# Layer 1 steps: parts split in fewer operations, sums on GpSimd, scalings on ScalarE, VectorE's additions in other steps

## What is computed

```
x = x + gb0 * gate * expert_out[slot]                      # end of layer 0
h = layernorm(x) * (1 + ca) + sa
k, v, q = split(h @ w_in);  a = softmax(q k^T / sqrt(8) + bias(rel. position)) v     # first attention, 16 heads
a, g = split(a @ w_gate + b_gate);  x = x + ga * a * sigmoid(g)
h = layernorm(x) * (1 + cb) + sb                           # the middle norm
h = h + mla(rmsnorm(h, g1))                                # second attention: causal, 16 heads, latent 64
h = h + moe(rmsnorm(h, g2))                                # top 2 of 8 experts
x = x + gb * h
```

## Time and profile before

| | us |
|---|---|
| median of three runs | 1864.76 (1862.15 to 1874.69) |
| the profiled execution | 1861.73 |
| its span, first to last instruction | 1860.0 |
| layer 1's first row minimum, stretch s = 0 | 693.1 |
| start of stretches s = 1 to 7 | 761.7, 840.8, 942.6, 1058.1, 1176.8, 1305.1, 1440.7 |
| last tile of stream 0 | 1570.7 |

### The profile page before, as it was taken

The page is one execution under the profiler, slowest core; times in us unless marked ns, Lnnn a source line. Parts: engine busy times, 40 slices in busy tenths (PEclk is TensorE's granted clock), DMA queues, the critical chain, the costliest instruction groups (busy, mean ns, idle before and its releaser), DMA issues.

```text
span 1860.0 us, 50554 instructions
## 1 busy us (share of the span) xinstructions
PE 1617.7 (87%) x19264; PEld 1179.7 (63%) x19264; DVE 1326.5 (71%) x4176; ACT 1007.1 (54%) x2196; POOL 779.3 (42%) x1021
## 2 busy tenths in 40 slices
PE   3899898899883939989999999989999988888887
PEld 2677676777772727766666666656767766544545
DVE  6678777876761127788778798897886786685646
ACT  1545454455451316665666667666666656564532
POOL 3111311220115237786656566565464574243210
PEclk7899999999995969999999999999999999988999
DMA  3631122122004424344423325143452333535321
GB/s 111 190 94 46 40 84 65 36 69 82 5 7 122 157 81 155 131 151 151 160 64 128 125 84 164 56 147 98 131 161 88 114 127 111 161 98 162 109 62 53
DMA packets 143839, 194.53 MB, mean 105 GB/s; under 512 B 21920, under 2 KB 110176, under 8 KB 142320
## 3 DMA queue, kind: packets, MB, share of 16 engines
q1 hardware_dynamic: 129312, 171.75, 29.6%
q0 software_dynamic: 5760, 14.03, 2.4%
q10 hardware_dynamic: 8528, 5.51, 1.0%
HBM read 142.39 MB, written 50.69 MB: 104 GB/s over the span
## 4 chain that ended last, share of the span: by engine, by line
PE 44%; DVE 9%; issue 7%; ACT 5%; DMA 1%; POOL 1%; SPq 0%; another core or an unknown queue 0%; ACTq 0%; POOLq 0%; DVEq 0%
PE ps L2350 9%; PE ps L2333 7%; PE ps L2384 6%; PE ps L2394 3%; DVE l_XY L2601 3%; PE ps L2361 3%; ACT PT L2162 2%; PE ps L1229 2%; PE ps L2484 2%; PE ps L1238 2%; PE ps L2459 2%; PE ps L2410 2%; DVE ps L2601 1%; PE ps L2431 1%; PE ps L2522 1%
## 5 line engine op out<-in xcount | busy, mean ns | idle before, releaser
L2053 POOL TENSOR_SCALAR l_XY<-l_XY,l_nmax 128x512 f32<-128x512 f32 x512 | 374.9, 737 | 295.9 <-DVE l_nmax L2601 287.6
L2601 DVE CUSTOM_DVE_ANT_0 l_XY<-ps,strips 128x512 f32<-128x512 f32 x512 | 347.7, 687 | 170.4 <-PE ps L2333 115.2
L2162 ACT ACTIVATE PT<-ps 128x512 f32<-128x512 f32 x512 | 307.3, 601 | 248.0 <-PE ps L2350 236.3
L2333 PE MATMUL ps<-l_stack 72*128 72x512 bf16 (+3 forms) x1024 | 350.9, 348 | 50.1 <-DVE l_nmax L2601 35.5
L2350 PE MATMUL ps<-ident,l_XY 128*128 128x128 f32 x2048 | 320.6, 279 | 1.7 <-ACT PT L2162 1.4
L2350 PEld LDWEIGHTS ps<-ident,l_XY 128*128 128x128 f32 x2048 | 236.9, 142 | 91.0 <-issue 56.8
L2601 DVE CUSTOM_DVE_ANT_0 ps<-ps,mask 128x384 f32<-128x384 f32 (+3 forms) x512 | 250.2, 496 | 24.3 <-PE ps L2333 20.2
L2361 PE MATMUL ps<-l_stack 75*128 75x256 bf16 (+3 forms) x512 | 157.2, 308 | 22.0 <-ACT PT_odd L2165 7.5
L2333 PEld LDWEIGHTS ps<-l_stack 72*128 72x128 bf16 x1024 | 101.1, 99 | 100.5 <-DVE l_nmax L2601 55.7
L2384 PE MATMUL ps<-PT,v_aug 128*10 128x128 f32 x4096 | 137.6, 275 | 6.8 <-ACT l_O_sb L2171 6.4
L2165 ACT ACTIVATE PT_even<-ps 128x512 f32<-128x512 f32 (+1 forms) x256 | 125.1, 494 | 22.8 <-PE ps L2363 17.3
(11 more groups left out here) (372 smaller groups left out, 3215.9 us busy)
## 6 DMA issues: line engine op xcount, KB each, us to landing
l_stack<-parts_dram SPq DMA_DIRECT2D x384, 96.0 KB
strips<-bias_dram SPq DMA_DIRECT2D x16, 1792.0 KB
stack<-parts_dram SPq DMA_DIRECT2D x48, 384.0 KB
w_own<-table_dram SPq DMA_DIRECT2D x60, 256.0 KB
parts_dram<-l_parts SPq DMA_DIRECT2D x32, 384.0 KB
rows_dram<-mask SPq DMA_DIRECT2D x6, 2048.0 KB, 8.9
parts_dram<-parts SPq DMA_DIRECT2D x16, 384.0 KB, 6.5
x_b<-rows_dram SPq DMA_DIRECT2D x72, 64.0 KB
```

The source lines that it names most:

```text
L2053: nc.gpsimd.tensor_scalar(XY[:, c % XY_BUFS], XY[:, c % XY_BUFS], -1.0, nmax[:, c % 8:c % 8 + 1], ALU.mult, ALU.add).then_inc(y_pool, 1)
L2162: nc.scalar.activation(PT[:, u % QUADS, j], src.rearrange("p (k q) -> p k q", q=P), ACT.Exp).then_inc(moved, 1)
L2333: nc.tensor.matmul(ps[:, n % 3, 0:w], stack[0:STACK, 0, h, q * P:(q + 1) * P], stack[0:STACK, 1, h, 0:w], start=True, stop=True).then_inc( ...
L2601: nc.vector.tensor_tensor_reduce(out=dst, in0=src, in1=add, scale=-1.0, scalar=3.0e38, op0=ALU.add, op1=ALU.min, accum_out=low).then_inc(s ...
```

## The change

- `pre` gets its steps from a new function `pre_step`: y0 * gate * gb0 in two halves at i = 57 and 61 of the stretch before (-7 and -3), the sum into x at 0 on GpSimd (`x_added`), statistics at 5, variance at 9, the root at 10, the normalisation at 13, the turn at 15. Batch 1 has steps of its own, batch 0 runs ahead of the loop as before (`first_pre`).
- Splitting: VectorE's one subtraction writes part 1 in bf16 directly (for pre at 24 and 27, for mid at 49 and 53); the casts go. GpSimd makes the float difference itself and then part 2 (`last_part`, two operations, the second waiting for the first; for pre at 26 and 29, for mid at 51 and 55). Only the very first batch keeps the old form.
- `mid`: the sum into x at 27 goes to GpSimd (`x_gated`), VectorE waits for it at 29. The layer norm and its rows become two fused operations, (x - mean) * row at 33 and h * rstd + row at 37, each as four of 128x128; the one at 35 goes, and the root is waited for at 37. The scaling at 43 goes to ScalarE, four of 128x128.
- `router`: the scaling goes to ScalarE too (k = 13, four of 128x128; k = 11 for batches 4 and 5). In `MIXED_STAGES` add, square, variance and power come one step later, the plan's five steps at k = 45, 49, 53, 55, 57 (i = 25, 29, 33, 35, 37).
- SyncE loads the row gb0 of the batch after next at i = 20. Four semaphores of layer 0's experts, which end at 8 = E, serve the new waits.

```diff
@@ -1330,8 +1331,8 @@
-MIXED_STAGES = dict(wo=1, add=3, square=5, var=8, power=9, scale=15, turn=17, logits=19, top0=21, top1=25, both=25, gap=27, count=28,
-                    place=37, gates=37, scatter=38, plan=(50, 52, 54, 56, 58), fold=41)
+MIXED_STAGES = dict(wo=1, add=4, square=6, var=9, power=10, scale=13, turn=17, logits=19, top0=21, top1=25, both=25, gap=27, count=28,
+                    place=37, gates=37, scatter=38, plan=(45, 49, 53, 55, 57), fold=41)
@@ -1389,6 +1390,13 @@
 def router_steps(b):
     return max(routing(b)["fold"], routing(b)["plan"][-1]) + 1
+def pre_step(b, stage):
+    if b == 1:
+        return {"y0": 3, "y1": 5, "x": 7, "statistics": 9, "var": 11, "power": 12, "xn": 13, "split": 24}[stage]
+    return TILES * (b - 1) + {"y0": -7, "y1": -3, "x": 0, "statistics": 5, "var": 9, "power": 10, "xn": 13, "split": 24}[stage]
...
+MADE_AT = [(-1, ("xp", 0))] + [(pre_step(b, "xn"), ("xp", b)) for b in range(1, B)] + [
+ROOTS_AT = [(TILES * s + 43, ("xm", b)) for s, b in MID_OF.items()] + [(MOE_START[b] + routing(b)["scale"], ("xf", b)) for b in range(ROUTED)]
+TOKENS_SCALED = {what: n for n, (_, what) in enumerate(sorted(ROOTS_AT))}
+VARIANCE_AT = [(-1, (0, 0))] + [(pre_step(b, "var"), (0, b)) for b in range(1, B)] + [
...
@@ -1552,7 +1561,7 @@
-        for off, name in ((14, "xp"), (20, "pq"), (22, "pk"), (23, "pv")):
+        for off, name in ((15, "xp"), (20, "pq"), (22, "pk"), (23, "pv")):
@@ -1986,7 +1996,7 @@
-                    if pre is not None and pre < B - 1 and i == 60:
+                    if pre is not None and pre < B - 1 and i == 20:
@@ -2098,8 +2108,18 @@
                     nc.gpsimd.tensor_tensor(rows, rows, bc(b_gate_sb[:].unsqueeze(1), [P, 2, 2 * C]), ALU.add).then_inc(gated_ready, 1)
+                def x_added(b):
+                    pool.wait_ge(y_scaled, E + b)
+                    nc.gpsimd.tensor_tensor(x_rows(b), x_rows(b), y0[:], ALU.add).then_inc(x_in, 1)
+                def x_gated(b):
+                    pool.wait_ge(mid_sum, E + b + 1)
+                    nc.gpsimd.tensor_tensor(x_rows(b), x_rows(b), h_of(b), ALU.add).then_inc(x_mid, 1)
                 def last_part(k, a, b):
+                    if PART_NO[a, b]:
+                        order.link(nc.gpsimd.tensor_tensor(qk[:, k, :], qk[:, k, :], parts[:, k, 0, :], ALU.subtract))
@@ -2108,6 +2128,9 @@
                     last_part(k, 0, 0)
                 gather(1, range(TT))
+                    for b in range(1, B):
+                        if m == pre_step(b, "x"):
+                            x_added(b)
@@ -2115,8 +2138,10 @@
-                    if pre is not None and i == 10:
+                    if pre is not None and m == pre_step(pre, "power"):
+                    if mid is not None and i == 27:
+                        x_gated(mid)
@@ -2127,9 +2152,9 @@
                         if mid is not None and i == 19 + half_:
                             gate_sum(mid, half_)
-                        if pre is not None and i == 25 + 4 * k:
+                        if pre is not None and i == 26 + 3 * k:
-                        if mid is not None and i == 52 + 4 * k:
+                        if mid is not None and i == 51 + 4 * k:
@@ -2293,9 +2318,17 @@
                         evacuate(*what)
                     for what in outs_at(m):
+                    if s in MID_OF and i == 43:
+                        b = MID_OF[s]
+                        act.wait_ge(rstd_ready, VARIANCES[2, b] + 1)
+                        for t in range(TT):
+                            last = nc.scalar.activation(xn[:, t, :], h_of(b)[:, t, :], ACT.Copy, scale=rstd[2][:, t:t + 1])
+                        last.then_inc(tok_scaled, 1)
                     if s in MID_OF and i == 39:
+                        if ("xm", b) in XN_BEFORE:
+                            act.wait_ge(turned, XN_BEFORE["xm", b] + 1)
@@ -2307,6 +2340,11 @@
                         if k == routing(b)["gap"]:
                             gap_exponent(b)
+                        if k == routing(b)["scale"]:
+                            act.wait_ge(rstd_ready, VARIANCES[3, b] + 1)
+                            for t in range(TT):
+                                last = nc.scalar.activation(xf[:, t, :], h_of(b)[:, t, :], ACT.Copy, scale=rstd[3][:, t:t + 1])
+                            last.then_inc(tok_scaled, 1)
@@ -2421,7 +2459,10 @@
-                        pe.wait_ge(tok_ready, TOKENS_MADE[name, k] + 1)
+                        if (name, k) in TOKENS_SCALED:
+                            pe.wait_ge(tok_scaled, E + TOKENS_SCALED[name, k] + 1)
+                        else:
+                            pe.wait_ge(tok_ready, TOKENS_MADE[name, k] + 1)
@@ -2647,38 +2688,56 @@
                 def split(k, a, b, part):
 
                     if part == 0:
-                        s = PART_NO[a, b]
-                        link(nc.vector.tensor_tensor(qk[:, k, :], qk[:, k, :], parts[:, k, 0, :], ALU.subtract))
+                        if PART_NO[a, b]:
+                            nc.vector.tensor_tensor(parts[:, k, 1, :], qk[:, k, :], parts[:, k, 0, :], ALU.subtract).then_inc(second_part, 1)
+                        else:
+                            link(nc.vector.tensor_tensor(qk[:, k, :], qk[:, k, :], parts[:, k, 0, :], ALU.subtract))
-                def pre(b, i):
-                    if i == 3:
+                def scaled(b, half_):
+                    if half_ == 0:
-                        for t in range(TT):
-                            last = nc.vector.scalar_tensor_tensor(out=y0[:, t, :], in0=y0[:, t, :],
-                                                                  scalar=gate_keep[:, b * TT + t:b * TT + t + 1],
-                                                                  in1=gb0_now[:], op0=ALU.mult, op1=ALU.mult)
-                        link(last)
-                    if i == 7:
-                        linked()
-                        ins = nc.vector.tensor_tensor(x_rows(b), x_rows(b), y0[:], ALU.add)
-                        ins.then_inc(x_in, 1)
-                    if i == 9:
+                    for t in (2 * half_, 2 * half_ + 1):
+                        last = nc.vector.scalar_tensor_tensor(out=y0[:, t, :], in0=y0[:, t, :],
+                                                              scalar=gate_keep[:, b * TT + t:b * TT + t + 1],
+                                                              in1=gb0_now[:], op0=ALU.mult, op1=ALU.mult)
+                    return last
+                def first_pre():
+                    scaled(0, 0)
+                    link(scaled(0, 1))
+                    linked()
+                    nc.vector.tensor_tensor(x_rows(0), x_rows(0), y0[:], ALU.add).then_inc(x_in, 1)
+                    dve.wait_ge(x_in, 1)
+                    statistics(0, 0)
+                    linked()
+                    variance(0)
+                    normalised(0, 0).then_inc(tok_ready, 1)
+                    for k in range(2):
+                        for part in range(2):
+                            split(k, 0, 0, part)
+                def pre(b, m):
+                    if m == pre_step(b, "y0"):
+                        scaled(b, 0)
+                    if m == pre_step(b, "y1"):
+                        scaled(b, 1).then_inc(y_scaled, 1)
+                    if m == pre_step(b, "statistics"):
                         statistics(0, b)
-                    if i == 9:
+                    if m == pre_step(b, "var"):
-                    if i == 11:
+                    if m == pre_step(b, "xn"):
-                    for at, k, part in ((22, 0, 0), (24, 0, 1), (26, 1, 0), (28, 1, 1)):
-                        if i == at:
-                            split(k, 0, b, part)
+                    for k in range(2):
+                        if m == pre_step(b, "split") + 3 * k:
+                            split(k, 0, b, 0)
@@ -2691,35 +2750,33 @@
-                        link(nc.vector.scalar_tensor_tensor(out=h, in0=h, scalar=0.5, in1=row(mid_rows[:, 0]),
-                                                            op0=ALU.mult, op1=ALU.mult))
-                    if i == 27:
-                        linked()
-                        link(nc.vector.tensor_tensor(x_rows(b), x_rows(b), h, ALU.add))
+                        nc.vector.scalar_tensor_tensor(out=h, in0=h, scalar=0.5, in1=row(mid_rows[:, 0]),
+                                                       op0=ALU.mult, op1=ALU.mult).then_inc(mid_sum, 1)
-                        linked()
+                        dve.wait_ge(x_mid, E + b + 1)
-                        wait_xn(("xm", b))
-                        link(normalised(1, b))
-                    if i == 35:
-                        linked()
-                        link(nc.vector.tensor_tensor(h, xn[:], row(mid_rows[:, 2]), ALU.mult))
+                        dve.wait_ge(var_ready, VARIANCES[1, b] + 1)
+                        for t in range(TT):
```

(29 more changed lines are left out.)

7 lines of the change are left out of this document (3 added, 4 removed).

## The result

| | before | after |
|---|---|---|
| median, us (11 runs each, one chip) | 1869.49 | 1882.06 (1877.27 to 1888.68) |
| ratio, 95% interval | | 1.0074 (1.0056 to 1.0093) |
| span of the profiled execution | 1860.0 | 1880.3 |
| last tile of stream 0 | 1570.7 | 1585.8 |

The change costs 12.6 us (1882.06 - 1869.49). I had forecast 9 us less than before, and 1882 lies above my range of 1840 to 1873.

The account below looks back on a forecast made before the run. TensorE sets the pace in layer 1, interrupted by VectorE where it has more to do. 4.9 + 11.8 + 0.5 - 2.0 - 2.0 - 5.0 = 8.2 us won: 1853.5 profiled, median forecast 1856 us, range 1840 to 1873.

Parts of the forecast that it names:

- ScalarE at 43: Mid norm's scaling on ScalarE, unsheltered at step 43: TensorE loses 0.25 us in each of 8 batches, 2.0 us.
- The pre moves: Next batch's preparation, steps 3 to 12: 9.7 us of TensorE's loss won, 4.8 lost anew, net 4.9 us won.
- Parts and fused norm: Steps 22 to 38, split without casts and fused middle norm: half of TensorE's 23.5 us loss won, 11.8 us.
- the term's lower end: Steps 22 to 38: nothing won if the remaining peaks stay as they are; the upper end was 22 us.
- 0.5 us for two things: Casts at 51 and 55 and scaling at 43 and 59 leave VectorE, which has room there: 0.5 us won.
- my sign for a late root: TensorE's waits for ScalarE's exponentials after step 43 growing by more than 0.5 us per batch mean the root came late.
- "Free" at step 57: Router's scaling on ScalarE at step 57 costs nothing, as ScalarE idles there behind the values matmuls.
- GpSimd's queue: Added GpSimd operations in steps 26 to 29 make TensorE wait 0.5 us in four stretches with scatters: 2 us lost.
- the rival: GpSimd becomes the bound, steps 26 to 33, past 4.3 us of lag: 21 us slower, 1886 us; chance 0.14.
- Blocking of VectorE: Three added GpSimd operations delay VectorE's two-input instructions 0.25 us each in 7 stretches: 5 us lost, upper bound 16.
- Order and queues: SyncE's earlier row load and the parts' stores, 1.2 us later of some 20 steps to the stacks' use: no cost.

Follow-up runs that it names:

- e8: Kernel before with only the fused middle norm (two fused operations at steps 33 and 37): ratio 0.9990 to the kernel before.
- e12: Kernel before without VectorE's two casts per split and with nobody making the float difference, so its third part is not right: ratio 0.9981.
- e4: Kernel before with only the steps of the next batch's preparation moved, the sum into x left on VectorE: ratio 0.9979.
- e1: Changed kernel with the scaling of step 43 back on VectorE as one 128x512 product: ratio 1.0030 to the kernel before.
- e16: Changed kernel with ScalarE's scaling at step 45 instead of 43 and the turn of xn at 46 instead of 45: ratio 1.0041.
- e10: Kernel before with the preparation's moves, the fused middle norm and the router's changes (scaling on ScalarE, sum, square, variance and root a step later): ratio 0.9967.
- e15: e9 with the router's sum, squares, variance and root one step later and its scaling on VectorE at 57: ratio 0.9968 to the kernel before.
- e14: Changed kernel with the scaling at 43 on VectorE and SyncE's store of the last batch's parts at step 42: ratio 1.0002 to the kernel before.
- e13: Second run of the same kernel as e9 (preparation's moves and fused middle norm only): ratio 0.9956 to the kernel before.
- e5: Kernel before with GpSimd's part subtraction done twice each time, all else as before: ratio 1.0051.
- e11: Changed kernel with SyncE storing the last batch's parts at step 42 instead of 30: ratio 1.0030 to the kernel before.
- e7: Changed kernel with the scaling at 43, the split parts and both sums into x back on VectorE as before: ratio 0.9980 to the kernel before.
- e18: e9 with SyncE's store of the last batch's parts at step 42 instead of 30: ratio 0.9920 to the kernel before.
- e9: Kernel before with the preparation's steps moved and the fused middle norm, nothing else: ratio 0.9917.
- e17: e9 with the preparation's normalisation at step 12 instead of 13: ratio 0.9948 to the kernel before.
- e2: Changed kernel with the split parts as before (float subtraction and cast on VectorE, one GpSimd operation, old steps): ratio 1.0002 to the kernel before.

## Why the prediction was wrong

Between 8.2 us won and 12.6 lost lie 20.8 us. The steps that failed, largest first: SyncE's queue, priced at nothing and worth 8.2 us; the parts with the fused norm, 11.8 us in the sum and about 5.4 measured (1.9 in e8, 3.5 in e12); ScalarE at 43, 2.0 in the sum and 8.2 measured; the router's shifted steps, not priced, 2.2 to 2.5. GpSimd's lag and the blocking of VectorE, 7.0 us together in the sum, lie inside the 3 to 10 that the runs leave for them, but that is luck, since neither was right by itself.

**The pre moves (4.9 us won): right.** e4 measures 3.9 (0.6 to 7.5). The inside differs: steps 3 to 12 gave back all 9.7 us in s = 1 to 6 and statistics at 5 cost nothing, but the normalisation at 13 costs more than my 0.3 us, 1.8 in s = 0 and 1 and 0.8 in s = 2.

**Parts and fused norm (11.8 us): mis-sized by a factor of two.** I took half of the loss in steps 22 to 38. Freed of the casts alone they gained 1.3 us (e12), of the norm's instructions alone 3.3 (e8). The peaks ahead of the casts' gain stayed, as the term's lower end said: steps 22 to 27 took 85.3 us over the eight stretches before and 85.1 in e12, and the gain came at 28 to 31. In 49 to 56, where I had 0.5 us for two things, the casts were worth 1.7.

**ScalarE at 43 (2.0 us): a factor of four too small,** 8.2 us (e1). I scaled from the squares at 39, where TensorE had some reserve; the row to go by was the block's own length (4 x 306 ns) against the distance to the next bank that TensorE needs. That nothing shelters step 43 was right, and e16 shows what shelter is worth. The root was in time, so my sign for a late root, a wait of more than 0.5 us, pointed at the wrong cause. "Free" at step 57 was right (e10 and e15).

**Not priced at all: the router's steps one later.** That put ScalarE's squares from 49, behind values, to 50: 0.6 us in each of four stretches, 2.5 us (e15).

**GpSimd's queue (2.0 us): the rival came true in kind, not in price.** I wrote that it decides past a lag of 4.3 us; the traces show 5.2, 4.3 and 4.2. Its price of 3.6 us for each stretch was too high, as the lag was worked off by step 36: e14 against e13 leaves 8.6 us, 5.0 of them in steps 22 to 38. Nor did the rival name the two largest losses, ScalarE at 43 and the rows behind SyncE's store. e5 shows that one operation more at steps 25, 29, 52 and 56 is enough to cost 9.5 us.

**Blocking of VectorE (5.0 us, bound 16): there, but elsewhere, and less.** I had looked at the subtraction and the product at 25. The subtraction went from 848 to 896 ns (22 of them, +1.1 us), the product from 1428 to 1092 (6, -2.0 us). What grew is the division's product of 128x128, which now meets GpSimd's added operations at steps 25 and 29. After, 841 to 1580 us, and its shortest, median and longest in the whole run:

```profile
L2654 DVE TENSOR_TENSOR l_o_tok<-l_o_raw,l_orec 128x128 f32<-128x128 f32 x45 | 23.9, 531 | 1.5
```

```profile
L2654 DVE TENSOR_TENSOR l_o_tok<-l_o_raw,l_orec x64: 291/382/1967, 728.8 to 1830.7; 128x128 f32<-128x128 f32 x64
```

Before it was this:

```profile
L2613 DVE TENSOR_TENSOR l_o_tok<-l_o_raw,l_orec 128x128 f32<-128x128 f32 x45 | 20.1, 447 | 1.5
```

That is 3.8 us more, so 2.9 us of VectorE's time in all, and no run separates what TensorE felt of it. The longest stands in step 25 of stretch 5, where it took 1967 ns against 291 at best:

```profile
1225.65 1.97 DVE L2654 TENSOR_TENSOR l_o_tok<-l_o_raw,l_orec 128x128 f32<-128x128 f32 x1
```

```profile
1224.99 1.36 POOL L2063 TENSOR_SCALAR l_XY<-l_XY,l_nmax 128x512 f32<-128x512 f32 x2
1226.32 1.15 POOL L2122 TENSOR_TENSOR l_qk<-l_qk,l_parts 128x512 f32<-128x512 f32 x1
```

GpSimd's added subtraction (L2122) ends at 1227.47 and the product at 1227.62, 0.15 us later. The same 0.15 us lie between the two ends at step 25 of stretch 4 (1109.01 and 1109.16) and at step 29 of stretch 3 (1000.28 and 1000.43). The Trainium skill (SBUF — State Buffer, "Who interferes with whom") says that a VectorE instruction with two SBUF inputs contends with a GpSimd instruction that reads SBUF. The trace agrees: both operations have two SBUF inputs, and VectorE's ended only once GpSimd's had. My error was to count added GpSimd operations times a mean wait. Where the two meet depends on the order, and e5, with 22 GpSimd operations more, lengthened the division's product by 1.3 us in all (476 ns) and none of the three instructions that I had named.

**Order and queues (nothing): wrong, and costly.** I gave the stores of the parts "1.2 us of some 20 steps to the stacks' use" and so looked at the stacks. Behind the store in SyncE's queue stood also the rows of an expert block, which in the kernel before were issued 7.6 us ahead of their use and take about that long. GpSimd's 3.7 us of delay (end of the second part 65.4 us into the stretch instead of 61.7) became 5.3 us of TensorE's waiting and a fallen clock: 8.2 us (e11). I had asked what stands behind SyncE's row load, and not what stands behind its store. Not all of the 8.2 us is GpSimd's doing: in e7, e10 and e13, whose GpSimd has nothing added, TensorE still waited 2.5, 2.2 and 2.0 us for these rows, and the clock fell. Against e13 the late rows cost 5.1 us in that piece (29.6 and 24.5).

**The sum again:** 3.9 (e4) + 1.9 (e8) + 3.5 (e12) won, 8.2 (ScalarE) + 8.2 (SyncE) + 2.2 (squares, e15 against e13) lost, and GpSimd's lag. The first six give 9.3 us lost against 12.6 measured, and leave about 3 us for the lag alone; by e14 it would be 8.6 - 2.2 + 3.5 = 9.9. The costs do not add exactly (e14 recovers 13.5 of 16.4), so I put the lag at 3 to 10 us; with 5 us of uncertainty in each difference, that is an estimate and not a measurement.

## What to carry to other kernels

Work taken off an engine is worth only what another engine waited for in that very step, and work put on an engine costs by what is queued behind it there, which can be a DMA queue three hops away; follow each queue to the next consumer without margin. The place of a block in the step pattern counts more than its length: four ScalarE instructions cost 1.1 us behind a light step and 0.2 us or less behind a heavy one. To find such costs, undo one part at a time and compare pieces of the schedule, which mostly repeat within 0.2 us where whole runs vary by 0.4%; and look at the granted clock of a piece before you explain its length.

## What the runs showed of the hardware

**The clock fell in the middle of a busy kernel, and the length of the wait ahead of it did not decide.** After's steps 22 to 38 in the stretch of 1179 took 38.8 us, where before took 36.1, although TensorE idled about as long in both (6.1 and 6.7 us). TensorE waited for VectorE once for 2.31 us and once for 1.69, and at each the granted clock fell:

```profile
1230.83 0.23 PE L2371 MATMUL ps<-l_stack 72*128 72x128 bf16 x1 [2.31 <-DVE l_nmax L2642]
...
1247.76 0.34 PE L2371 MATMUL ps<-l_stack 72*128 72x384 bf16 x1 [1.69 <-DVE l_nmax L2642]
```

```profile
1228.00:1231.00 3.00, 0.69 (x7) 0.31 (x5) 2.90 (x11) 0.96 (x3) 2.38 (x3) 1.00 0.01 4
1231.00:1234.00 3.00, 3.00 (x16) 2.59 (x16) 2.70 (x7) 1.68 (x4) 2.92 (x3) 0.54 0.27 88
...
1249.00:1252.00 3.00, 3.00 (x13) 1.94 (x12) 2.93 (x12) 1.70 (x4) 1.27 (x2) 0.50 0.58 191
```

Before had no single wait over 1.42 us there and kept 1.00 throughout; its busy time in the piece is 29.46 us, after's 32.70 at a mean clock of 0.87. e1, with after's steps there and 0.95, took 37.0 us and 29.71 busy. The 2.31 us came behind the product of 1.97 us shown above and 2 us of the plan's work, which now stands at step 25.

But the same wait can end either way. A wait of 1.42 or 1.43 us near step 31 of stretch 5 stands in nine profiles. Behind it the clock fell in e4, e8, e10, e15 and e18 and stayed at 1.00 in before, e9, e13 and e17. The windows from the end of this wait, e8 first, then e9:

```profile
1225.11:1227.11 2.00, 1.75 (x17) 1.11 (x21) 1.97 (x13) 1.09 (x2) 1.74 (x2) 1.00 0.40 129
1227.11:1230.61 3.50, 3.50 (x46) 2.34 (x38) 3.41 (x11) 0.51 (x1) 2.60 (x3) 0.51 0.45 146
```

```profile
1233.71:1235.71 2.00, 1.75 (x17) 1.11 (x21) 1.97 (x13) 1.09 (x2) 1.74 (x2) 1.00 0.39 125
1235.71:1239.21 3.50, 3.19 (x55) 2.28 (x46) 3.46 (x12) 1.57 (x4) 2.60 (x3) 1.00 0.47 155
```

And e11's clock fell for some 10 us behind waits of only 0.56 and 0.47 us. Steps 49 to 56 of stretch 5, e11 and after:

```profile
1276.34:1300.23 23.89, 22.84 (x179) 15.35 (x180) 12.08 (x38) 13.56 (x34) 11.75 (x14) 0.79 0.21 64
```

```profile
1277.11:1296.86 19.75, 18.33 (x179) 12.15 (x180) 12.11 (x38) 13.37 (x34) 11.76 (x14) 1.00 0.25 76
```

Of the ten waits of 1.98 us and more for a block's rows in stretch 6, nine had a fallen clock with them; in e2, with 2.48 us, it stayed at 1.00. So long waits are to be shunned, but what decides is open, and a fallen clock can add 3 to 4 us to a piece in one profile of a kernel and nothing in the next.

**The rows of a block (two transfers of 64 KB) took 7.2 (e15) to 9.2 us (e7) from issue to use where TensorE waited for them in stretch 6,** behind the stack and strip loads issued just before; in e9 and e13, the same kernel, 7.4 and 8.7. Why it differs stays open, as does why e14's costs fall short of their sum.
